# Layer one's last tile of every second chunk selected by TensorE, coefficients kept for eight chunks, degrees summed on VectorE

## The chip, the cores and the metric

One NeuronCore of a Trainium2 chip runs the kernel; nothing is shared with other cores. The metric is the device time of one execution in microseconds, lower is better. Each quoted median is over several executions of the same program on one chip; the profile is one further execution, with its own time.

## What is computed

A graph network over 3125 nodes with 128 features and 100000 edges, sorted by destination. After a layer norm and a relu, two relational layers run one after the other: an edge gathers the row of its source node, weighs it by eight coefficients (one for each basis, from its type, times the edge's norm), and the rows are summed by destination; a dense product with eight basis matrices and a loop weight follows. Then two plain graph convolutions use the edge counts and the degrees of the nodes.

```python
def _rel_layer(h, src, dst, etype, norm, V, comp, loop_w, bias, activation):
    c = comp[etype]
    for b in range(num_bases):                 # 8 bases
        xb = h @ V[b]
        m = m + c[:, b, None] * xb[src]
    agg = segment_sum(m * norm, dst)
    out = agg + bias + h @ loop_w
...
deg = segment_sum(ones, dst)                   # for the two convolutions
norm = rsqrt(deg)[src] * rsqrt(deg)[dst]
```

## The kernel before, in words

Nodes lie in 25 groups of 128. The edges lie in 784 tiles of 128 (782 real ones), eight tiles to a chunk, 98 chunks, four chunks to a group. `relational_layer` is called twice. In the code the first call has `layer == 0`; the texts here call it layer one, and the second call (`layer == 1`) layer two. Every engine runs its own program over groups and chunks, and semaphores join them. Work on an engine is in the order in which the code issues it.

In layer one, for each chunk c = 4g + j:

- GpSimd (L765) starts an indirect DMA for each tile, which fetches 128 rows of `h` into `ring`, a buffer of eight chunks. Before a chunk it waits until TensorE has used the chunk that lay in that slot (`edges_done`). 32 tiles are fetched ahead of the layer, in `prepare` (L280).
- SyncE loads the edge types for a chunk six ahead (`co.load`, L456), and in chunk j = 1 of each group it stores the finished group's slab of edge counts, 800 KB (`store_slab`, L793).
- VectorE builds, in this order: the one-hots of types for chunk c + 6 (L464), the matches of destinations (L868), the one-hots of the source's place in its block (`build_lo`, L874), the weighted matches `C` (`weigh`, L888), the one-hots of block and destination `M` (`build_keys`, L879), and the coefficients of chunk c + 5 (`co.scale`, L479 and L483). `build_lo` waits for TensorE to have begun chunk c - 1 (`m_free`); TensorE waits for `M` of chunk c (`m_ready`), so VectorE is at most one chunk ahead. `keep_deg` (L935) copies a group's degrees in chunk j = 2.
- TensorE first has two register loads (L1100, L1102), then the slab part `sum_slab` (L1002, L1033, L1038, L1041: edge counts in two halves), the coefficient product (L473), and then the edge part (L1124: 16 recorded passes of the gathered rows against `C`, after a wait for the rows' landing and for `c_ready`) with the hand-over to the next bank (L1002 of `ps_z`, L1129). In chunk j = 1, between the register loads and the slab part, `out_and_deg` multiplies the last group's sums by the eight bases (L552 to L554) and sums its degrees by 25 small matmuls of the fp16 counts with ones (L1068). At the end of chunk j = 3 there is one transposition (L543).
- ScalarE copies both sums out of PSUM (L1174, L1184), and finishes the group (L568, L570).

Layer two has a feature that layer one lacks. Of every chunk up to number 87 only seven tiles are gathered. The eighth is selected: SyncE loads its 128 source numbers to all partitions (`load_sources`), VectorE builds 25 blocks of one-hots in two halves (`make_pick`, L910), TensorE multiplies them with the rows of `H`, split once into three bf16 parts by `split_rows` (L897 to L900) (`pick_rows`, L1083: 25 matmuls of 384 columns into one bank), and VectorE adds the three parts into the ring (`keep_picked`, L916).

All coefficients of both layers are made in layer one and lie in two tables of 784 tiles.

## Time and profile before

| | us |
|---|---|
| median of 3 runs | 2128.14 (2127.25 to 2131.23) |
| the profiled execution | 2125.18 |
| its span in the trace | 2123.6 |

| engine | busy us | share of the span |
|---|---|---|
| TensorE (PE) | 1806.7 | 85% |
| its weight loads (PEld) | 1346.7 | 63% |
| GpSimd (POOL) | 1453.1 | 68% |
| VectorE (DVE) | 1190.5 | 56% |
| ScalarE (ACT) | 360.4 | 17% |

The profiled execution took 1.6 us more than its span, and lies 3 us under the median. Layer one runs from about 90 us to 1068 us, layer two from there to about 2020 us, and a short dense stage ends the kernel.
### The profile page before, as it was taken

To read this page: it belongs to the slowest core of one execution; us is meant where nothing else is said; L and a number is where in the kernel's file an instruction comes from. 1 tells how busy PE (TensorE), PEld (TensorE's weight loads), DVE (VectorE), ACT (ScalarE), POOL (GpSimd) and SP (SyncE) were. 2 spreads that over 40 slices of the span, in tenths; PEclk is the share of its full clock that TensorE was granted. 3 is DMA by queue.
4 is the path that set the end of the run, shared out by engine and by line. 5 is a ranking of instruction groups with operands and counts; after the bars stand their busy time and mean duration, and the time that the engine had idled before them with its cause. 6 is when DMAs were issued, how large, how long until landed. Compare 5 with 4: busy or idle time off the path is not lost. (4 is left out here: it accounts for less than half of the span.)

```text
span 2123.6 us, 38749 instructions
## 1 busy us (share of the span) xinstructions
PE 1806.7 (85%) x11730; PEld 1346.7 (63%) x11731; DVE 1190.5 (56%) x2013; ACT 360.4 (17%) x869; POOL 1453.1 (68%) x1573
## 2 busy tenths in 40 slices
PE   1398998989888888887849989889999899978798
PEld 1277777777666676766637766666666666655455
DVE  7565665656555554654267766666666756612433
ACT  2022222222222221222201101001010101101200
POOL 5777777777777777777567777777777777776000
PEclk8555555555555555555579989999999999979899
DMA  5233333232232223223222222223332232334363
GB/s 144 68 78 96 80 80 93 77 98 76 76 95 77 77 77 93 78 74 88 60 65 63 60 59 60 58 83 83 97 88 83 80 95 75 90 92 128 130 216 124
DMA packets 188885, 186.53 MB, mean 88 GB/s; under 512 B 109132, under 2 KB 161085, under 8 KB 188794
## 3 DMA queue, kind: packets, MB, share of 16 engines
q0 software_dynamic: 47232, 96.83, 17.1%
q1 hardware_dynamic: 133510, 84.47, 14.1%
q10 hardware_dynamic: 8052, 4.04, 0.7%
q8 instruction: 55, 0.90, 0.2%
q14 instruction: 36, 0.29, 0.0%
HBM read 159.75 MB, written 25.47 MB: 87 GB/s over the span
## 5 line engine op out<-in xcount | busy, mean ns | idle before, releaser
L765 POOL DMA_INDIRECT ring<-h_rows,rel_idx x1356 | 1305.5, 963 | 425.6 <-issue 394.8
L1124 PE MATMUL rel_ps_z<-rel_C,ring 128*128 128x56 f32 x3128 | 540.5, 346 | 79.7 <-DMA ring<-h_rows,rel_idx 79.2
L1124 PEld LDWEIGHTS rel_ps_z<-rel_C,ring 128*128 128x128 f32 x3128 | 524.8, 260 | 94.4 <-issue 90.4
L1083 PE MATMUL rel_ps_p<-rel_h_parts,rel_pick 128*128 128x384 bf16 x2200 | 391.8, 337 | 48.4 <-DVE rel_h_parts L900 22.0
L910 DVE TENSOR_TENSOR rel_pick<-rel_src_row,dve_bank 128x1664 bf16<-128x1664 int32 (+1 forms) x176 | 319.5, 1816 | 182.8 <-PE rel_ps_p L1083 180.2
L1083 PEld LDWEIGHTS rel_ps_p<-rel_h_parts,rel_pick 128*128 128x128 bf16 x2200 | 217.3, 101 | 200.6 <-issue 66.5
L1184 ACT ACTIVATE rel_ZT<-rel_ps_z 128x304 f32 x292 | 114.2, 426 | 1071.2 <-PE rel_ps_z L1124 1065.7
L874 DVE TENSOR_TENSOR rel_lo<-dve_bank,src_lo_table 128x1024 bf16<-128x1024 f32 x98 | 120.0, 1225 | 235.2 <-PE rel_ps_a L1033 234.8
L1174 ACT ACTIVATE rel_A<-rel_ps_a 128x500 f32 x292 | 165.6, 603 | 454.4 <-PE rel_ps_a L1041 419.9
L464 DVE TENSOR_SCALAR rel_onehot<-rel_types,type_id 100x1024 bf16<-100x1024 uint8 x196 | 141.6, 764 | 166.1 <-DMA rel_types<-edge_types 163.0
L552 PE MATMUL rel_ps_o<-V,rel_ZT 128*128 128x128 f32 x784 | 142.4, 356 | 65.4 <-issue 62.3
L552 PEld LDWEIGHTS rel_ps_o<-V,rel_ZT 128*128 128x128 f32 x784 | 132.5, 264 | 67.3 <-issue 63.7
L879 DVE TENSOR_TENSOR rel_M<-dve_bank,key_table 128x1400 bf16<-128x1400 f32 x98 | 157.4, 1606 | 0.0
L1041 PE MATMUL rel_ps_a<-rel_M,rel_lo 128*128 128x175 bf16 x784 | 153.2, 353 | 1.8 <-DVE rel_M L879 1.8
L888 DVE TENSOR_TENSOR rel_C<-dve_bank,coef 128x448 f32<-128x448 f32 x196 | 121.5, 620 | 34.1 <-PE rel_ps_z L1129 20.7
L473 PE MATMUL rel_ps<-comp_parts,rel_onehot 100*128 100x48 bf16 x1568 | 78.6, 211 | 56.0 <-DVE rel_onehot L464 47.9
L774 POOL DMA_INDIRECT ring<-h_rows,idx_table x88 | 89.7, 1019 | 52.4 <-issue 28.3
L1002 PE MATMUL rel_ps_a<-zero 1*128 1x500 bf16 x196 | 108.3, 553 | 15.0 <-issue 14.9
L473 PEld LDWEIGHTS rel_ps<-comp_parts,rel_onehot 100*128 100x128 bf16 x1568 | 79.2, 118 | 57.5 <-DVE rel_onehot L464 48.2
L1129 PEld LDWEIGHTS rel_ps_z<-rel_C,ring 128*128 128x128 f32 x388 | 78.4, 252 | 39.7 <-issue 26.9
L1015 PE MATMUL rel_ps_early<-early_slot,hp_parts 128*128 128x512 f16 (+1 forms) x441 | 100.4, 388 | 3.0 <-DVE early_sums L931 2.4
L1129 PE MATMUL rel_ps_z<-rel_C,ring 128*128 x388 | 96.5, 322 | 0.0
(206 smaller groups left out, 1282.9 us busy)
## 6 DMA issues: line engine op xcount, KB each, us to landing
ring<-h_rows,rel_idx POOLq DMA_INDIRECT x1356
A_slabs<-rel_A SPq DMA_DIRECT2D x25, 800.0 KB
A_slot<-A_slabs SPq DMA_DIRECT2D x25, 800.0 KB, 4.4
early_slot<-A_slabs SPq DMA_DIRECT2D x18, 896.0 KB, 6.1
rel_types<-edge_types SPq DMA_DIRECT2D x97, 100.0 KB
rel_src_row<-in_src_dram SPq DMA_DIRECT2D x88, 64.0 KB, 3.1
last_slot<-A_slabs SPq DMA_DIRECT2D x4, 512.0 KB, 6.1
ring<-h_rows,idx_table POOLq DMA_INDIRECT x120
```

Of the source, the lines that this page charges most:

```text
L464: ins = self.nc.vector.tensor_scalar(self.onehot[:, s % 2, h, :], self.etype[:, s % 2, :], self.t.type_id[0:RH, h:h + 1], None, ALU.is_equal)
L473: ins = self.nc.tensor.matmul(self.ps[:, e * 6 * NB:(e + 1) * 6 * NB], self.onehot[:, s, h, e * P:(e + 1) * P], flat(self.t.comp[:, h, :, ...
L552: m.matmul(self.bank(g)[:, 0:P], ZT[:, b, :], t.V[self.layer][:, b, :], start=(b == 0), stop=False)
L765: g_.indirect_dma_start(ring[:, s * CHUNK + i, :], None, rows_in, bass.IndirectOffsetOnAxis(ap=idx[which][:, n:n + 1], axis=0)).then_inc(l ...
L879: v.tensor_tensor(M[s][:, :, :], keys.unsqueeze(1).to_broadcast(shape), t.key[:, bass.ds(c * CHUNK, CHUNK)].unsqueeze(2).to_broadcast(shap ...
L888: v.tensor_tensor(C[s][:, :, :, :], match[s].unsqueeze(2).to_broadcast(shape), t.coef[layer][:, bass.ds(c * CHUNK, CHUNK), :].unsqueeze(3) ...
L910: v.tensor_tensor(pick[:, b0:b0 + n, :], src_row[s][:, :].unsqueeze(1).to_broadcast(shape), node_ids[:, b0:b0 + n].unsqueeze(2).to_broadca ...
L1041: ins = m_.matmul(into[:, :, bass.ds(half_at[h][i], TW)], lo[s][:, h * HALF + i, :], keyed(s, h * HALF + i), start=False, stop=(i == HALF ...
L1083: ins = m_.matmul(ps_p[s][:, 0:3 * P], pick[:, b, :], h_parts[:, b, :, :].rearrange("p c n -> p (c n)"), start=(b == 0), stop=(b == SRC_BL ...
L1124: ins = m_.matmul(bank(ps_z[s], NB)[:, :, bass.ds(at[i], TW)], ring[:, first + i, :], C[s][:, i, :, :], start=False, stop=(i == n - 1))
L1129: m_.matmul(bank(ps_z[1 - s], NB)[:, :, 0:1], ring[:, first + CHUNK - 1, :], C[s][:, CHUNK - 1, :, bass.ds(at[CHUNK], 1)], start=False, st ...
L1174: ins = s_.activation(A[into][:, :, bass.ds(column, HN)], half_bank(ps_a[h]), ACT.Copy)
```

## The change

In layer one the last tile of each odd chunk from 5 to 95 (46 of them) is no longer gathered but selected as in layer two: with two buffers for source numbers in place of four, and one PSUM bank. TensorE does the 25 matmuls for chunk c + 1 in the even chunk c, between the coefficient product and the edge part, and its last edge matmul of chunk c + 1 waits for the selected row (`row_ready`). VectorE splits `H` in group 0 (two pieces of five groups in each of the chunks 0 and 1, one in chunk 2), builds one half of the one-hots in the odd chunk before and the other in the even chunk, and adds the three parts in the odd chunk. SyncE loads the source numbers a group ahead, behind a wait for the one-hots made from that buffer (`pick_ready`) and ahead of the slab's store and the next types.

To make room, layer one's coefficients are kept in a ring of eight chunks, and the bank `ps_o` becomes the last quarter of the bank `ps_h`. The 25 small matmuls for the degrees are replaced: VectorE reduces the group's counts over the 25 blocks (3200 fp16 numbers in each partition) at the end of its chunk j = 1, and TensorE does one fp32 matmul of that sum with ones at the start of chunk j = 2. `keep_deg` moves from j = 2 to j = 3, and the last two groups' degrees come after the loop.

```diff
-    def scale(self, eng, m):
+    def scale(self, eng, m, slot=None):
...
+            into = self.t.coef[l][:, bass.ds(m * ET if l or slot is None else slot * ET, ET), :]
...
-        self.ps_o = ctx.enter_context(nc.psum_tensor(f"{name}_ps_o", [P, 512], F32))
+        self.ps_o = self.ps_h[:, 3 * P:4 * P] if layer == 0 and not whole else ctx.enter_context(nc.psum_tensor(f"{name}_ps_o", [P, 512], F32))
...
+        def first_picks(c):
+
+            return isinstance(c, int) and FIRST_PICK <= c < END_PICK and c % 2 == 1
+
+        def number(g, j):
+
+            return 2 * g - 2 + j // 2
+
+        def gathers(s, late=False):
+
+            return CHUNK if late else CHUNK - (1 if layer == 1 else s % 2)
...
-                for i in range(CHUNK if late else GATHERS):
+                for i in range(gathers(s, late)):
...
+                def load_sources(g, j):
+
+                    k, s = number(g + 1, j), j // 2
+                    after(sp, pick_ready, 2 * k - 2)
...
+                        if j % 2 == 1 and not (isinstance(g, int) and not first_picks((g + 1) * CPG + j)):
+                            load_sources(g, j)
...
+            def sum_degrees(q, parity):
+                dve.wait_ge(a_kept, (q * CPG + (CPG + 1)) * 2 if not is_group(q, GROUPS - 1) else HALVES)
+                after(dve, deg_done, q)
+                v.tensor_reduce(deg_sum[:, :], A[parity][:, :, MARGIN:MARGIN + P].rearrange("p b n -> p n b"), AX.X, ALU.add).then_inc(deg_summed, 1)
...
                     if layer == 0:
                         match_nodes(c, s)
+                        if j % 2 == 0 and not (isinstance(g, int) and not first_picks(c + 1)):
+                            make_pick(number(g, j + 1), j // 2, g - 1, (1,))
                         build_lo(c, s)
-                        weigh(c, s)
+                        weigh(c, s, parity * CPG + j)
                         build_keys(c, s)
+                        if is_first and j < 3:
+                            split_rows(split_chains, ((0, 1), (2, 3), (4,))[j])
+                        if j % 2 == 1:
+                            if not (isinstance(g, int) and not first_picks(c)):
+                                keep_picked(number(g, j), 0, (parity * CPG + j) * CHUNK + CHUNK - 1)
+                            ahead = (g, 3) if j == 1 else (g + 1, 1)
+                            if not (isinstance(g, int) and not first_picks(c + 2)):
+                                make_pick(number(*ahead), ahead[1] // 2, ahead[0] - 1, (0,))
...
+                    if layer == 0 and j == 1 and not is_first and not is_last:
+                        sum_degrees(g - 1, 1 - parity)
+                    if layer == 0 and j == 3 and not is_first:
                         keep_deg(g - 1)
...
             if layer == 0:
-                keep_deg(GROUPS - 2)
-                keep_deg(GROUPS - 1)
+                for q in (GROUPS - 2, GROUPS - 1):
+                    sum_degrees(q, q % 2)
+                    keep_deg(q)
...
+            def degrees(q):
+                pe.wait_ge(deg_summed, q + 1)
+                after(pe, deg_kept, q)
+                pe.wait_ge(fin.h_new, min(q + 2, GROUPS) if isinstance(q, int) and q >= GROUPS - 2 else q + 1)
+                m_.matmul(fin.ps_h[:, 2 * P:2 * P + 1], deg_sum[:, :], t.ones[:, 0:1], start=True, stop=True).then_inc(deg_done, 1)
...
                     if layer == 0 and j == 1 and not is_first and not is_last:
-                        out_and_deg(g - 1, 1 - parity)
+                        out(g - 1, 1 - parity)
+                    if layer == 0 and j == 2 and not is_first:
+                        degrees(g - 1)
...
+                    if layer == 0 and j % 2 == 0 and not (isinstance(g, int) and not first_picks(c + 1)):
+                        if is_group(g, 1) and j == 0:
+                            pe.wait_ge(split_done, GROUPS // SPLIT_GROUPS)
+                        pick_rows(number(g, j + 1), 0)
...
+                        if layer == 0 and i == CHUNK - 1 and j % 2 == 1 and not (isinstance(c, int) and not first_picks(c)):
+                            pe.wait_ge(row_ready, number(g, j) + 1)
...
-                        t.coef[0] = left(first_layer, "coef0", [P, TILES, NB], F32)
+                        t.coef[0] = left(first_layer, "coef0", [P, COEF_RING * CHUNK, NB], F32)
```

## Rows read from the trace of the kernel before

**Rows 1.** The page's 40 slices of the span, tenths busy.

```profile
POOL 5777777777777777777567777777777777776000
PEclk8555555555555555555579989999999999979899
```

**Rows 2.** Windows: length; PE, PEld, DVE, ACT, POOL busy us (count); clock; DMA share, GB/s.

```profile
139.00:515.00 376.00, 343.91 (x2341) 280.46 (x2340) 226.44 (x370) 97.77 (x210) 284.21 (x301) 0.56 0.33 85
559.00:1016.00 457.00, 386.85 (x2556) 312.30 (x2554) 243.91 (x398) 107.52 (x231) 347.62 (x368) 0.54 0.31 81
```

**Rows 3.** TensorE's waits, 139 to 515, then 559 to 1016: total us, times, longest.

```profile
PE rel_ps_o L552 <- issue: 28.1, 10, 2.9
...
PE rel_ps_z L1124 <- DMA ring<-h_rows,rel_idx: 34.4, 17, 6.6
```

**Rows 4.** GpSimd's groups of instructions by line, 559 to 1016.

```profile
L765 POOL DMA_INDIRECT ring<-h_rows,rel_idx x352 | 344.4, 978 | 109.6 <-issue 100.8 <-DMA ring<-h_rows,rel_idx 7.0 <-PE rel_ps_z L1129 1.8
```

**Rows 5.** Timeline, TensorE in chunk 1, chunk 97, and VectorE's last degrees: start, length.

```profile
100.35 0.23 PE L1033 MATMUL rel_ps_a<-rel_M,rel_lo 128*128 x1
...
1057.95 0.22 PE L1033 MATMUL rel_ps_a<-rel_M,rel_lo 128*128 x1
...
1068.16 0.16 DVE L935 TENSOR_SCALAR deg<-rel_ps_h 128x1 f32<-128x1 f32 x1 [14.95 <-PE rel_ps_h L1068]
```

**Rows 6.** Timeline of TensorE, from an edge part j = 0 through chunk j = 2.

```profile
464.63 3.64 PE L1124 MATMUL rel_ps_z<-rel_C,ring 128*128 128x56 f32 x16
...
471.96 3.75 PE L552 MATMUL rel_ps_o<-V,rel_ZT 128*128 128x128 f32 x16 [2.80 <-issue]
...
476.36 0.78 PE L1068 MATMUL rel_ps_h<-ones,rel_A 128*128 128x1 f16 x25
477.07 0.38 PE L1002 MATMUL rel_ps_a<-zero 1*128 1x500 bf16 x1
...
478.98 3.49 PE L1124 MATMUL rel_ps_z<-rel_C,ring 128*128 128x56 f32 x16
...
483.29 0.59 PE L1002 MATMUL rel_ps_a<-zero 1*128 1x500 bf16 x1
...
486.53 3.64 PE L1124 MATMUL rel_ps_z<-rel_C,ring 128*128 128x56 f32 x16
...
491.23 0.59 PE L1002 MATMUL rel_ps_a<-zero 1*128 1x500 bf16 x1 [0.18 <-issue]
```

**Rows 7.** Windows: an unbroken stretch of layer one, then of layer two's first selection.

```profile
484.00:488.00 4.00, 4.00 (x34) 3.22 (x32) 3.74 (x4) 1.21 (x2) 3.08 (x4) 0.50 0.35 91
...
1093.00:1097.00 4.00, 4.00 (x13) 1.87 (x14) 0.62 (x1) 0.00 (x0) 3.09 (x4) 0.50 0.16 45
1097.00:1101.00 4.00, 2.13 (x13) 1.08 (x11) 1.83 (x2) 0.00 (x0) 3.08 (x4) 1.00 0.22 57
```

**Rows 8.** Timeline: the first two selections of layer two on TensorE.

```profile
1092.94 6.19 PE L1083 MATMUL rel_ps_p<-rel_h_parts,rel_pick 128*128 128x384 bf16 x25 [22.01 <-DVE rel_h_parts L900]
...
1101.58 4.24 PE L1083 MATMUL rel_ps_p<-rel_h_parts,rel_pick 128*128 128x384 bf16 x25 [2.45 <-DVE rel_pick L910]
```

**Rows 9.** Timeline: an edge part of layer one at the full clock, next chunk's start.

```profile
684.26 1.97 PE L1124 MATMUL rel_ps_z<-rel_C,ring 128*128 128x56 f32 x16
...
688.01 0.59 PE L1002 MATMUL rel_ps_a<-zero 1*128 1x500 bf16 x1 [1.24 <-issue]
```

**Rows 10.** Timeline of VectorE: one-hots, the three parts' sum; groups: a split.

```profile
1099.17 0.56 DVE L916 TENSOR_REDUCE ring<-rel_ps_p 128x128 f32<-128x384 f32 x1 [5.54 <-PE rel_ps_p L1083]
1099.64 3.54 DVE L910 TENSOR_TENSOR rel_pick<-rel_src_row,dve_bank 128x1664 bf16<-128x1664 int32 x2
...
L898 DVE TENSOR_TENSOR dst_table<-H,rel_h_parts 128x640 f32<-128x640 f32 x5 | 4.1, 824 | 0.2
```

**Rows 11.** A long reduction (in `prepare`), and VectorE's types, 139 to 515, by line.

```profile
44.85 2.69 DVE L425 TENSOR_REDUCE pre_bad<-pre_wrong 1x1 f32<-1x2450 f32 x1
...
L464 DVE TENSOR_SCALAR rel_onehot<-rel_types,type_id 100x1024 bf16<-100x1024 uint8 x80 | 57.9, 765 | 73.3 <-DMA rel_types<-edge_types 72.0 <-issue 1.2
```

More of the change, by code:

```diff
@@ L730, in half_bank, with landings @@
             return b[:, 0:SRC_BLOCKS * HN].rearrange("p (a n) -> p a n", n=HN)
-        GATHERS = CHUNK - layer
-        def landings(half, late):
+        def first_picks(c):
[4 more added lines that the diff above has]
+            return CHUNK if late else CHUNK - (1 if layer == 1 else s % 2)
+        def landings(half, s, late=False):
             if layer == 1 and late:
-                return PICKED // 2 * (GATHERS * 16) + (half - PICKED // 2) * (CHUNK * 16)
-            return half * (GATHERS * 16)
+                return PICKED // 2 * (gathers(s) * 16) + (half - PICKED // 2) * (CHUNK * 16)
+            if layer == 0 and s % 2 == 1:
+                return half * (CHUNK * 16) if isinstance(half, int) and half < 3 else half * (gathers(s) * 16) + 2 * 16
+            return half * (gathers(s) * 16)
         @block.gpsimd
@@ L754, in chunk @@
                 landed = (ring_even, ring_odd)[s % 2]
-                hold(pool, landed, landings(m * (SLOTS_RING // 2) + s // 2, late))
+                hold(pool, landed, landings(m * (SLOTS_RING // 2) + s // 2, s, late))
                 if s in (0, 2, 4):
@@ L769, in _ @@
                 landed = (ring_even, ring_odd)[c % 2]
-                hold(pool, landed, c // 2 * GATHERS * 16)
+                hold(pool, landed, landings(c // 2, c))
                 if c == SLOTS_RING - 2:
                     stage(0, SLOTS_RING)
-                for i in range(c * CHUNK, c * CHUNK + GATHERS):
+                for i in range(c * CHUNK, c * CHUNK + gathers(c)):
                     g_.indirect_dma_start(ring[:, i, :], None, rows_in, bass.IndirectOffsetOnAxis(ap=t.idx[:, i:i + 1], axis=0))\
@@ L940, in _ @@
                 make_pick(0, 0, 0)
-                split_rows()
+                split_rows(split_chains, range(GROUPS // SPLIT_GROUPS))
                 match_nodes(0, 0)
@@ L1145, in _ @@
             groups(pe, group)
-            out_and_deg(GROUPS - 1, (GROUPS - 1) % 2)
+            out(GROUPS - 1, (GROUPS - 1) % 2)
+            if layer == 0:
+                degrees(GROUPS - 2)
+                degrees(GROUPS - 1)
             if layer == 1:
```

60 lines of the change are left out of this document (32 added, 28 removed).

## The prediction, made before the changed kernel ran

> **What bounds the kernel now.** I read the page's slices first. In layer one (the first twenty slices) GpSimd stands at an even 7 tenths and TensorE's granted clock at 5 tenths, in layer two at 8 to 9 [rows 1]. The two windows over layer one then show that it isn't one regime [rows 2]. Between 139 and 515 us TensorE passes ten groups in 376 us, 37.6 us each (the ten waits ahead of L552, one for each group, count them); from 559 to 1016 us it takes 457 us for the 352 gathers of eleven groups, 41.5 us each [rows 3, 4]. TensorE's waits say why. In the first stretch it never waits for gathered rows for long enough to be listed; in the second it does so 17 times, 34.4 us in all, which is most of the 11 x 3.9 = 43 us between the regimes [rows 3]. GpSimd meanwhile starts one gather after another: idle time before them is "issue", and a gather costs 457 / 352 = 1.30 us in all [rows 4]. It had chunks in hand when the layer began, TensorE worked that lead off at 37.6 us a group, and since about 530 us GpSimd sets the pace. So the gathers that the change removes are a bound only while TensorE can do a group in less than GpSimd's new time, 30 x 1.30 = 39.0 us. TensorE has 39.0 - 37.6 = 1.4 us a group to spare for two selections, at its present clock. That is the question of the case.
>
> **TensorE's group, part by part** [rows 6]. At 1.2 GHz a slab part with the coefficient product takes 486.53 - 483.29 = 3.2 us, and the edge part until the next chunk begins 491.23 - 486.53 = 4.7 us. The dense product takes 476.36 - 471.96 = 4.4 us, after which the slab part runs at 2.4 GHz and takes 1.9 us (477.07 to 478.98). From the edge part of j = 0 to the dense product pass 7.3 us, of which 2.8 us are idle, "issue": the two register loads stand there while the slab's store is on the DMA queues.
>
> What the change adds and takes there, for each of the 23 groups with selections:
>
> - Two selections. One took 4.2 us at the full clock, and the very first of layer two, which began after an idle stretch, 6.2 us: 13 of its matmuls began in 4 us at 0.50, then the clock was full [rows 7, 8]. All 25 at 0.50 would be 25 x 4 / 13 = 7.7 us. In layer one the engine comes from an edge part that leaves the clock at 1.2 GHz, but the slab part is dense and stands right ahead of the selection. I take the half of that first cold stretch: 2 us for 6 matmuls and 19 at 4.2 / 25 = 0.17, that is 5.2, and 10.4 for two. Bounds 4.2 and 7.7 each.
> - The 25 degree matmuls go: 477.07 - 476.36 = 0.7 us; one fp32 matmul of one column comes, two passes; sixteen passes of 128 columns took 3.75, so two take 0.47 at most, and I take 0.3. Net -0.4.
> - Behind a selection the clock is high. The edge part until the next chunk was 3.75 us at the full clock, of which 1.2 us was "issue" (the register loads now show) [rows 9]. In j = 2 that saves 0.9 us. In j = 0 the same, and the register loads come some 5 us later, towards the end of the slab's store: I take 4.8 us in place of 7.3, -2.5 (bounds 0 and -3.6).
> - For a clock that holds into the next slab part now and then: -0.7 (bounds 0 and -2.6, both slab parts behind a selection at 1.9).
>
> Sum: 37.6 + 10.4 - 0.4 - 0.9 - 2.5 - 0.7 = 43.5 us a group. This is over GpSimd's 39.0, so GpSimd fills its ring and waits for `edges_done`; its 46 spared gathers, 46 x 1.30 = 60 us, are then worth nothing. TensorE's wait for landed rows disappears too, but the time is spent.
>
> **VectorE** was busy 226.4 us in ten groups, 22.6 each [rows 2]. Per group come two pairs of one-hot halves, 2 x 3.54, two sums of three parts, 2 x 0.56 [rows 10], and the degree reduction. No row shows that one; the nearest reduces 2450 numbers in 2.69 us [rows 11], so 3200 take about 3.5 (2.7 if fp16 were quicker by a quarter, 5 if the strided read cost half as much again). Sum 34.3 us, under 43.5. What could make it late is its waits: 7.2 us a group for the types, which queue behind the slab's store [rows 11]. The reduction, one sum and one one-hot half (5.8 us) stand in just that stretch, after `M` of j = 1 and before the one-hots of types, so most of this wait is filled. `keep_picked` in an odd chunk waits for TensorE's selection, and behind it are queued the next one-hot half, the coefficients and the next `build_lo`; TensorE has an edge part and a slab part to do in that time, some 7 us, against some 7 us of VectorE's work. I cost it at nothing, with a bound of 2 us a group. The wait of TensorE for the summed degrees stands ahead of the slab part of j = 2, which waits for `M` of that chunk, made later on the same engine: nothing. `keep_deg` one chunk later is still a chunk ahead of the transposition that waits for it: nothing. SyncE's loads of source numbers (64 KB) stand ahead of the slab's store; the one-hots they wait for were made half a group earlier, and ScalarE's copies of the slab come later anyway: nothing, bound 1 us. The ring of coefficients changes an address, and the shared bank is guarded by waits on copies done two chunks earlier: nothing. ScalarE's wait for the split in group 0: nothing.
>
> **Once.** In group 0 VectorE does five splits of four instructions, 20 x 0.82 = 16.4 us [rows 10], two of them (6.6 us) in each of chunks 0 and 1. With 5.7 us of its own work a chunk it needs 12.3 us where TensorE needs 8: 4.3 us late twice and 1 to 2 us in chunk 2, about 10 us (bounds 5 and 14). At the end of the layer the last group's reduction runs only after the last dense product, since the one buffer must be free: 3.5 us, a matmul and its copy, less the 25 small matmuls, about +4.5 ahead of what follows VectorE's last degrees [rows 5].
>
> **Sum.** Before, chunk 1 to chunk 97 (24 groups) took 1057.95 - 100.35 = 957.6 us [rows 5]. After: 37.6 + 10 for the first and 23 x 43.5 = 1000.5, together 1048.1; +90.5, and +4.5 at the end: +95.0. Layer two and the dense stage keep their code and their data. The profiled execution took 2125.2 (1.6 over its span, 3 under the median of the runs), so 2125.2 + 95.0 = 2220.2. I forecast 2220.
>
> **Rule against row.** TensorE's matmuls fill 4.00 of 4.00 us in the middle of chunk j = 2, and the clock granted there is 0.50, while a selection lifts it from 0.50 to 1.00 [rows 7]. So being busy isn't what keeps the clock up here; edge parts, which mostly load weights for 56 columns, are busy at 1.2 GHz. The Trainium skill, "TensorE: Matmul & The Clock Gate" (section "Why this matters for your kernels"), advises to keep the engine continuously busy and free of idle gaps, to get and hold the full clock. By that rule TensorE, once it is never idle, would run at 2.4 GHz through the whole group; this is the first rival. The row of chunk j = 2 speaks against it.
>
> **Rivals.**
>
> 1. The clock stays up, and GpSimd remains the bound: not slower. Two dense selections a group would lift TensorE to 2.4 GHz for most of it. A group would then be 4 x 1.9 + 4 x 3.75 + 4.4 + 2 x 4.25 + 0.5 = 36.0 us, under 39.0. GpSimd's 46 gathers come off in full, 60 us, the split's 10 us are hidden in its lead, and the end costs 4.5: 2125.2 - 60 + 4.5 = 2070. For it: layer two, with a selection in each chunk, has 8 to 9 tenths [rows 1]. Against it: there a selection comes every chunk and no slab part is built; here an edge part of the odd chunk, at 1.2 GHz in every group of before, stands between. It decides where TensorE's group falls under (957.6 - 47.6 - 4.5) / 23 = 39.4 us, 4.1 under my sum. Chance 0.10, and 0.02 for a time within 0.2% of no change.
> 2. The clock is up around each selection and into the slab parts, but not throughout: 4.45 in place of 5.2 for each selection (-1.5), and both slab parts behind them at 1.9 in most groups (-2.6 in place of -0.7, of which I count -1.2): 43.5 - 2.7 = 40.8 us a group, -62 from the forecast: 2158. For it: a slab part at 1.9 us behind the dense product [rows 6]. Chance 0.13.
> 3. VectorE is late. If the 7.2 us for types stay, and each of the two `keep_picked` waits 2.5 us with work queued behind it, a group is 34.3 + 7.2 + 5 = 46.5 us: +69, 2289. It decides when its waits pass 43.5 - 34.3 = 9.2 us a group; before, it waited 15 us. Chance 0.07.
> 4. The selections run at 1.2 GHz throughout: 7.7 each, +5.0 a group, and the savings behind them (0.9 + 2.5 + 0.7) gone: 52.6, +209, 2429. Against it is the rise within the first selection of layer two [rows 7]. Chance 0.03.
>
> **How the numbers follow.** The forecast has 0.65, rivals 1 to 4 and no change 0.35. Its own bounds: selections at 6.2 give +2.3 a group, +53; at 4.5, -25; the group-0 and store terms +-30. With rival 2 below and the near half of rival 3 above, the range is 2140 to 2285; it leaves out rival 1, no change, rival 4 and part of rival 3, under 0.2. A measurement of this kernel can tell 0.2% (4 us) from no change. Faster by over that: 0.10; within: 0.02; slower: 0.88.
>
> **What the next profile would show.** Layer one ends at about 1163 us in place of 1068. TensorE's wait for landed rows is gone, and GpSimd waits for TensorE's L1129. The selections in layer one last 4.5 to 6 us, with the clock at 0.5 when they begin; the mean clock of the layer rises from 0.55 to 0.65 or more. VectorE is busy 34 us a group and its wait for types shrinks to 2 or 3 us. I would be wrong if TensorE's group took under 39.4 us, which a granted clock over 0.8 in the layer would show, or if VectorE's waits for the types and the selection added up to over 9 us a group.

## The result and the profile after

The changed kernel took 2316.77 us (median of 4 runs, 2311.72 to 2319.32) against 2128.76 for the kernel before beside it: a ratio of 1.088, 95% interval 1.086 to 1.090. The forecast was 2220 with a range of 2140 to 2285. It had the sign right and missed half of the size: +188 us in place of +92, 32 us beyond its range.

The profiled execution took 2319.32 us, its span is 2317.5. Two rows of its page's 40 slices, for [rows 1]:

```profile
POOL 6776656666566665566502777777777777777000
PEclk7566766666666666666675899988999999978899
```

GpSimd falls from 7 tenths to mostly 6 and 5 in layer one, the clock rises from 5 tenths to mostly 6. So the gathers went and, as the waits below show, no longer pace the layer. The waits of the whole layer (175 to 1190 us: total, times, longest), for [rows 3, 4]: TensorE's first, then VectorE's and GpSimd's.

```profile
PE rel_ps_h L555 <- issue: 59.0, 21, 3.1
PE rel_ps_a L1049 <- issue: 42.9, 21, 2.1
PE rel_ps_h L1116 <- ACT H L571: 1.1, 1, 1.1
PE rel_ps_a L1088 <- DVE rel_M L906: 0.8, 1, 0.8
...
DVE ring L945 <- PE rel_ps_p L1131: 193.0, 43, 5.1
DVE rel_lo L901 <- PE rel_ps_a L1080: 34.5, 41, 3.4
...
POOL ring L782 <- PE rel_ps_z L1185: 47.1, 10, 5.3
```

(The last row is of 559 to 1016 us.) TensorE waits for no gathered row, and for VectorE 0.8 us in a thousand. What is left ahead of it are idle stretches that no semaphore explains ("issue"), now twice a group (L555 and L1049), 102 us in all. In the program's order TensorE's register loads stand there, as they do ahead of every chunk; that they are the cause is a reading, since the trace doesn't list them. VectorE and GpSimd wait for TensorE, so TensorE's own sequence sets the layer.

Where the 193.9 us between the spans stand, by the marks of [rows 5]: chunk 1 begins at 106.21 in place of 100.35 (+5.9); from there to chunk 97, at 1236.76, pass 1130.55 us in place of 957.6 (+172.9); from chunk 97 to VectorE's last degrees 17.9 in place of 10.2 (+7.7); behind them 1062.9 in place of 1055.4 (+7.4). The medians differ by 188.0, 5.9 less than these spans; in which stretch the two profiled executions differ from their medians isn't known. The first group took 45.8 us, so the other 23 took 1084.8 / 23 = 47.2 each, against a forecast of 43.5.

One of them, piece by piece, TensorE's timeline (start, length, idle time ahead of it), for [rows 6]:

```profile
609.51 5.19 PE L1131 MATMUL rel_ps_p<-rel_h_parts,rel_pick 128*128 128x384 bf16 x25
614.54 1.89 PE L1180 MATMUL rel_ps_z<-rel_C,ring 128*128 128x56 f32 x16
...
619.72 3.75 PE L555 MATMUL rel_ps_h<-V,rel_ZT 128*128 128x128 f32 x16 [2.74 <-issue]
...
624.41 0.62 PE L1049 MATMUL rel_ps_a<-zero 1*128 1x500 bf16 x1
...
627.68 3.64 PE L1180 MATMUL rel_ps_z<-rel_C,ring 128*128 128x56 f32 x16
...
632.25 0.56 PE L1116 MATMUL rel_ps_h<-ones,rel_deg_sum 128*128 128x1 f32 x2
632.74 0.59 PE L1049 MATMUL rel_ps_a<-zero 1*128 1x500 bf16 x1
...
635.97 5.61 PE L1131 MATMUL rel_ps_p<-rel_h_parts,rel_pick 128*128 128x384 bf16 x25
641.42 1.89 PE L1180 MATMUL rel_ps_z<-rel_C,ring 128*128 128x56 f32 x16
...
645.93 0.59 PE L1049 MATMUL rel_ps_a<-zero 1*128 1x500 bf16 x1 [2.08 <-issue]
```

| piece, start to start | before [rows 6] | after | difference | forecast |
|---|---|---|---|---|
| two selections | none | 5.03 + 5.45 | +10.5 | +10.4 |
| edges of j = 0, to the dense product | 7.33 | 5.18 | -2.15 | -2.5 |
| dense product | 4.40 | 4.69 | +0.3 | 0 |
| degrees (25 small matmuls, then one) | 0.71 | 0.49 | -0.2 | -0.4 |
| slab part of j = 1 | 1.91 | 3.27 | +1.35 | -0.7 |
| edges of j = 1 | 4.31 | 4.57 | +0.25 | with it |
| edges of j = 2 | 4.70 | 4.51 | -0.2 | -0.9 |
| sum | | | +9.8 | +5.9 |

The slab part of j = 1 had run at 2.4 GHz before [rows 6] and doesn't any more: of the first 22 groups it took 1.9 us in 19 before and in 2 after, 3.2 or 3.3 in the others. The windows show where the clock stands (length; TensorE and weight loads busy; VectorE, ScalarE, GpSimd; granted clock; DMA share, GB/s): first and second half of the selection, the edges behind it, the idle stretch, the dense product, the slab part of j = 1.

```profile
609.60:612.00 2.40, 2.40 (x13) 1.20 (x10) 0.85 (x1) 0.92 (x2) 1.79 (x3) 0.60 0.14 39
612.00:614.40 2.40, 2.40 (x17) 1.43 (x16) 0.00 (x0) 0.00 (x0) 1.79 (x3) 1.00 1.06 248
614.60:616.80 2.20, 2.20 (x20) 2.00 (x18) 2.06 (x2) 0.18 (x1) 1.40 (x2) 1.00 0.98 197
616.90:619.70 2.80, 0.08 (x1) 0.02 (x1) 2.66 (x5) 0.46 (x2) 1.37 (x2) 0.76 0.33 104
619.80:624.30 4.50, 4.50 (x20) 4.28 (x21) 4.50 (x2) 0.00 (x0) 3.28 (x5) 0.50 0.18 48
624.50:627.60 3.10, 3.10 (x28) 1.88 (x27) 3.10 (x5) 0.79 (x2) 2.49 (x3) 0.50 0.16 45
```

The clock is up from the middle of the selection and through the edges, 2.2 us of work. Then TensorE stands idle for 2.74 us, the clock falls within that stretch (0.76 over it), and all that follows until the next selection is at 1.2 GHz. An idle stretch of 2.80 us stands there in the kernel before too, and its dense product still ended with the clock up [rows 6]; why it doesn't after a selection isn't shown. The end of the layer, on VectorE, where the last reduction stands behind the last but one group's degrees:

```profile
1247.74 0.16 DVE L969 TENSOR_SCALAR deg<-rel_ps_h 128x1 f32<-128x1 f32 x1 [18.02 <-PE rel_ps_h L1116]
1247.82 6.13 DVE L965 TENSOR_REDUCE rel_deg_sum<-rel_A 128x128 f32<-128x3200 f16 x1
1254.63 0.16 DVE L969 TENSOR_SCALAR deg<-rel_ps_h 128x1 f32<-128x1 f32 x1 [0.68 <-PE rel_ps_h L1116]
```

### The profile page after: what moved, and what is told of

It reads as the page before. It is cut to its first block and busy times, and to the rows that moved or that the text cites. A ratio compares the mean times of both kernels' runs of the same rounds, so it can differ in the third digit from the quotient of the medians.

```text
span 2317.5 us, 40468 instructions
## 1 busy us (share of the span) xinstructions
PE 1983.8 (86%) x12305; PEld 1410.7 (61%) x12306; DVE 1534.7 (66%) x2196; ACT 360.0 (16%) x869; POOL 1406.5 (61%) x1527
## 5 line engine op out<-in xcount | busy, mean ns | idle before, releaser
L782 POOL DMA_INDIRECT ring<-h_rows,rel_idx x1312 | 1259.3, 960 | 531.4 <-issue 429.3
L1131 PE MATMUL rel_ps_p<-rel_h_parts,rel_pick 128*128 128x384 bf16 x3350 | 649.1, 357 | 48.8 <-DVE rel_h_parts L927 22.0
L939 DVE TENSOR_TENSOR rel_pick<-rel_src_row,dve_bank 128x1664 bf16<-128x1664 int32 (+1 forms) x268 | 486.0, 1814 | 182.3 <-PE rel_ps_p L1131 179.8
L1131 PEld LDWEIGHTS rel_ps_p<-rel_h_parts,rel_pick 128*128 128x128 bf16 x3350 | 348.1, 106 | 311.6 <-issue 134.8
L1180 PE MATMUL rel_ps_z<-rel_C,ring 128*128 128x56 f32 x3128 | 466.3, 314 | 38.4 <-DMA ring<-h_rows,rel_idx 38.4
L1180 PEld LDWEIGHTS rel_ps_z<-rel_C,ring 128*128 128x128 f32 x3128 | 459.9, 231 | 50.2 <-issue 42.8
L945 DVE TENSOR_REDUCE ring<-rel_ps_p 128x128 f32<-128x384 f32 x134 | 74.7, 557 | 218.0 <-PE rel_ps_p L1131 215.3
L1049 PE MATMUL rel_ps_a<-zero 1*128 1x500 bf16 x196 | 114.9, 586 | 51.9 <-issue 51.9
L965 DVE TENSOR_REDUCE rel_deg_sum<-rel_A 128x128 f32<-128x3200 f16 x25 | 153.5, 6140 | 0.0
L555 PE MATMUL rel_ps_h<-V,rel_ZT 128*128 128x128 f32 x400 | 93.0, 427 | 64.2 <-issue 63.4
L555 PEld LDWEIGHTS rel_ps_h<-V,rel_ZT 128*128 128x128 f32 x400 | 86.6, 329 | 65.8 <-issue 64.8
```

The source lines that it names most:

```text
L555: m.matmul(self.bank(g)[:, 0:P], ZT[:, b, :], t.V[self.layer][:, b, :], start=(b == 0), stop=False)
L782: g_.indirect_dma_start(ring[:, s * CHUNK + i, :], None, rows_in, bass.IndirectOffsetOnAxis(ap=idx[which][:, n:n + 1], axis=0)).then_inc(l ...
L939: v.tensor_tensor(pick[:, b0:b0 + n, :], src_row[s][:, :].unsqueeze(1).to_broadcast(shape), node_ids[:, b0:b0 + n].unsqueeze(2).to_broadca ...
L965: v.tensor_reduce(deg_sum[:, :], A[parity][:, :, MARGIN:MARGIN + P].rearrange("p b n -> p n b"), AX.X, ALU.add).then_inc(deg_summed, 1)
L1131: ins = m_.matmul(ps_p[s][:, 0:3 * P], pick[:, b, :], h_parts[:, b, :, :].rearrange("p c n -> p (c n)"), start=(b == 0), stop=(b == SRC_BL ...
L1180: ins = m_.matmul(bank(ps_z[s], NB)[:, :, bass.ds(at[i], TW)], ring[:, first + i, :], C[s][:, i, :, :], start=False, stop=(i == n - 1))
```

## The experiments

The theory after the result: TensorE's selections are nearly the whole loss, the reduction is no part of the pace, and the miss of 3.7 us a group comes from where the selection stands, ahead of an idle stretch that wastes the clock it wins. Its rivals: the reduction or the one-hots delay the group; or a selection costs TensorE its time wherever it stands.

Five runs were made where the kernel before takes 2127 to 2131 us; I tell these first. The first four stood beside the same runs of it (2131.45), u1 was made later beside others (2127.34). Group times are from the start of the dense product of group 0 to that of group 22, both read in the timeline, divided by 22; those of before are from its first profile.

| kernel | us | ratio to before, 95% | starts | group |
|---|---|---|---|---|
| before | 2131.45 | | 133.58, 1010.11 | 39.8 |
| r0, the change | 2320.51 | 1.089 [1.086, 1.092] | 147.34, 1194.49 | 47.6 |
| r1, no selection | 2141.27 | 1.004 [1.002, 1.006] | 133.76, 1012.68 | 40.0 |
| r2, degrees on TensorE | 2301.79 | 1.080 [1.078, 1.082] | 147.56, 1185.71 | 47.2 |
| r4, selections behind the edges | 2440.14 | 1.144 [1.142, 1.147] | 148.04, 1310.39 | 52.8 |
| u1, one late selection | 2119.45 | 0.996 [0.995, 0.998] | 148.87, 1007.56 | 39.0 |

**The change again (r0).**

> The changed kernel itself, unedited, as the measure that the three variants beside it are read against. If the chip behaves as in the first comparison, 2312 to 2320 us, a ratio of 1.086 to 1.090 to the kernel before, and groups of 47 to 48 us in layer one. In the four runs of the first set the kernel before itself took 2777 us instead of 2128, with long waits for signals of other engines in the trace; if that comes back, the ratio here tells whether the change costs the same share there: by the theory that TensorE alone sets the pace, the same 6.9 us a group more; by the rival that signals between engines set the pace on such a chip, much less, and the variants can't be told apart by it.

It came out as in the first comparison, 2320.51.

**No selection (r1).** The diff takes away what belongs to selections in layer one, the split of `H` in group 0 too, and leaves the ring of coefficients and the degree sum on VectorE.

```diff
-                        if j % 2 == 0 and not (isinstance(g, int) and not first_picks(c + 1)):
-                            make_pick(number(g, j + 1), j // 2, g - 1, (1,))
...
-                        pick_rows(number(g, j + 1), 0)
...
-            return CHUNK if late else CHUNK - (1 if layer == 1 else s % 2)
+            return CHUNK if late else CHUNK - layer
```

> The same source as e1_no_selection, run beside the change itself. No selection and no one-hots: GpSimd gathers all eight tiles of every chunk in layer one again; the degree sum stays on VectorE and the coefficients stay kept for eight chunks. Theory (the selections' time on TensorE is the cause of all the loss in layer one): the groups fall back to 40 to 40.6 us and the whole to 2132 to 2142 us, the 4 to 14 us above the kernel before being the two reductions at the end of the layer. Rival (the VectorE reduction, 6.14 us once a group, sits in the chain of every group): groups of 42 us or more, 2170 us or more.

2141.27, at the upper end of the theory's range, and far from the rival's 2170. So 179 of the 189 us are the selections with their split. TensorE's wait for gathered rows is back, as in [rows 3] (139 to 1016 us):

```profile
PE rel_ps_z L1160 <- DMA ring<-h_rows,rel_idx: 44.8, 26, 6.5
```

Of the 10 us above before, the reductions at the end of the layer are 8.2: from the start of the last dense product to the last degrees pass 13.0 us, against 4.8. The groups here also show that the fast slab part of j = 1 isn't lost to selections alone: without any, it took 3.3 us in 7 of the first 22.

**Degrees back on TensorE (r2).**

```diff
-                        sum_degrees(g - 1, 1 - parity)
...
+                for b in range(SRC_BLOCKS):
+                    ins = m_.matmul(fin.ps_h[:, 2 * P:2 * P + 1], A[parity][:, b, MARGIN:MARGIN + P], t.ones16[:, 0:1],
+                                    start=(b == 0), stop=(b == SRC_BLOCKS - 1))
```

> The same source as e2_degrees_on_pe, run beside the change itself. Both selections stay, the degrees of a group are summed on TensorE by its 25 small matmuls as in the kernel before, and VectorE's reduction is gone. Theory (TensorE sets the pace, the reduction is off the path except at the end of the layer): the groups stay at 47 to 48 us or grow by up to 0.9, the end of the layer is 7 us shorter, 2305 to 2330 us. Rival (the reduction delays the one-hots or the edges): groups of 44 us or less, 2230 us or less.

2301.79, 3 under the band I had given, and far from the rival. The reduction takes nothing from a typical group: in both kernels most alternate between 47.5 and 48.1 us. Of the 18.7 us the profiled executions show 5.6 at the end of the layer, 9.0 in the 22 groups and 1.2 behind the layer; the rest is between them and the medians. The middle one is a surprise of its own. Five of r2's groups took 44.4 to 46.4 us and all others 47.0 or more, against one of 44.8 in r0 (and two of 44.9 and 45.2 in the first profile of the change). Two groups of r2 in a row, the first short, the second long (dense product and the edges of j = 1):

```profile
236.77 3.50 PE L555 MATMUL rel_ps_h<-V,rel_ZT 128*128 128x128 f32 x16 [2.15 <-issue]
242.66 1.97 PE L1180 MATMUL rel_ps_z<-rel_C,ring 128*128 128x56 f32 x16
...
281.60 3.75 PE L555 MATMUL rel_ps_h<-V,rel_ZT 128*128 128x128 f32 x16 [2.57 <-issue]
289.56 3.64 PE L1180 MATMUL rel_ps_z<-rel_C,ring 128*128 128x56 f32 x16
```

The same instructions: in the short one the clock rises at the end of the dense product, and the edges take 1.97 us; in the long one it doesn't. From the dense product to these edges pass 5.9 or 8.0 us. The windows behind the two dense products (columns as above) have the clock at 1.00 and 0.50:

```profile
241.00:244.00 3.00, 3.00 (x40) 2.55 (x40) 2.71 (x3) 1.21 (x2) 2.39 (x3) 1.00 0.37 104
286.00:289.00 3.00, 3.00 (x16) 1.62 (x16) 1.78 (x3) 0.60 (x1) 2.39 (x3) 0.50 0.44 111
```

That is the clock at work, in one kernel, with nothing else changed; what tips it isn't shown. So one short group says little, and a kernel has to be judged by many.

**Both selections behind the edges (r4).** `pick_rows` moves from ahead of the edge part of an even chunk to behind it. In j = 0 the selection is then followed by the dense product, which the program issues at the start of j = 1 (the expectation puts it ahead of the selection, which is wrong).

```diff
-                    if layer == 0 and j % 2 == 0 and not (isinstance(g, int) and not first_picks(c + 1)):
-                        pick_rows(number(g, j + 1), 0)
                     s, n = sum_edges(g, c, j, at)
...
+                    if layer == 0 and j % 2 == 0 and not (isinstance(g, int) and not first_picks(c + 1)):
+                        pick_rows(number(g, j + 1), 0)
```

> The same source as e4_selection_after_edges, run beside the change itself. The same two selections, each at the end of the even chunk, behind its edge matmuls and dense product, not before them. Theory (of the 47.2 us of a group, about 3.7 come from the place of the selection: the clock that it wins is lost before the dense product and the next slab, and the register load behind it is waited for): groups of 43 to 45 us, 2215 to 2265 us. Rival (the 3.7 us come with a selection wherever it stands, since the sum of TensorE's work is longer and its clock lower): 46.5 us or more, 2300 us or more.

2440.14, 5 us a group slower than the change. By the number this is in the rival's range, but not by its cause, a selection's own time on TensorE. TensorE's waits (175 to 1190 us) show why, and VectorE's timeline where they come from.

```profile
PE rel_ps_a L1088 <- DVE rel_M L906: 126.7, 38, 5.6
PE rel_ps_h L1116 <- DVE rel_deg_sum L965: 43.7, 19, 2.8
PE rel_ps L475 <- DVE coef L486: 28.1, 20, 2.2
PE rel_ps_a L1049 <- issue: 10.1, 12, 1.1
PE rel_ps_h L555 <- issue: 6.6, 9, 0.9
...
615.45 1.60 DVE L906 TENSOR_TENSOR rel_M<-dve_bank,key_table 128x1400 bf16<-128x1400 f32 x1
624.60 0.56 DVE L945 TENSOR_REDUCE ring<-rel_ps_p 128x128 f32<-128x384 f32 x1 [7.55 <-PE rel_ps_p L1131]
...
627.90 6.16 DVE L965 TENSOR_REDUCE rel_deg_sum<-rel_A 128x128 f32<-128x3200 f16 x1
...
638.75 1.60 DVE L906 TENSOR_TENSOR rel_M<-dve_bank,key_table 128x1400 bf16<-128x1400 f32 x1
```

VectorE stands 7.6 us for the selected rows. Behind that wait it has queued the copy, the one-hots, the coefficients, the reduction and then the next masks `M`, which are ready 15.8 us after the selection ended; TensorE waits for them. A wait moved on one engine was moved on the other too, and there the reduction does count. The three waits are 198.5 us in 19.2 groups, 10.3 a group: without them 42.5, which is what the theory wanted, but that is a subtraction and no run. What the trace does show of the theory: the idle stretches ahead of L555 and L1049 are 16.7 us in place of the change's 102, each of the first 22 dense products took 2.4 or 2.5 us (4.7 in the change), and each slab part behind them 1.9 us.

**One late selection, degrees on TensorE (u1).** To take VectorE's queue out, one selection a group instead of two (chunk j = 1's, at the end of j = 0), and no reduction. GpSimd gathers 31 tiles of 32. Three things differ from the change at once, the number of selections, their place and the degrees; r2 prices the degrees, and the timeline has to tell the other two apart.

```diff
-            return isinstance(c, int) and FIRST_PICK <= c < END_PICK and c % 2 == 1
+            return isinstance(c, int) and FIRST_PICK <= c < END_PICK and c % CPG == 1
...
+                    if layer == 0 and j == 0 and not (isinstance(g, int) and not first_picks(c + 1)):
+                        pick_rows(number(g, j + 1), 0)
```

> The kernel of t2_one_late_pe_degrees again, alone, on the chance of a chip on which the kernel before takes 2131 us: theory, groups of about 38 us while TensorE sets the pace and 40.3 us once GpSimd does, 2100 to 2110 us in all; rival, 42.5 us a group or more, 2190 us or more. Where the kernel before takes 2700 us or more, again within 1% of it.

2119.45: faster than the kernel before by 0.4%, interval 0.2 to 0.5, and than the change by about 200 us. The rival (2190 or more) is out; the theory's 2100 to 2110 is missed by 9 us. TensorE's group is 39.0 us, 1.4 over the 37.6 of [rows 3], not 5 over it, where I had 38. GpSimd goes on without a pause and is only a little slower (355 gathers in the 457 us from 559 to 1016, 1.29 each, 39.9 for 31), so that TensorE never worked off its lead and waited for no gathered row. TensorE's timeline:

```profile
606.83 3.64 PE L1176 MATMUL rel_ps_z<-rel_C,ring 128*128 128x56 f32 x16
...
611.21 7.02 PE L1131 MATMUL rel_ps_p<-rel_h_parts,rel_pick 128*128 128x384 bf16 x25
618.06 1.95 PE L555 MATMUL rel_ps_h<-V,rel_ZT 128*128 128x128 f32 x16
...
620.49 0.37 PE L1046 MATMUL rel_ps_a<-zero 1*128 1x500 bf16 x1
...
622.41 1.97 PE L1176 MATMUL rel_ps_z<-rel_C,ring 128*128 128x56 f32 x16
...
626.29 0.76 PE L1114 MATMUL rel_ps_h<-ones,rel_A 128*128 128x1 f16 x25 [1.36 <-issue]
```

and its windows: most of the selection, then the dense product with the slab part.

```profile
613.50:617.50 4.00, 4.00 (x16) 1.95 (x15) 0.00 (x0) 0.00 (x0) 3.06 (x5) 0.57 0.45 116
618.00:622.00 4.00, 4.00 (x35) 3.17 (x34) 3.59 (x8) 0.45 (x1) 3.08 (x4) 1.00 0.21 50
```

This selection is itself slower than the change's, 6.85 us against 5.03, and gets the clock only near its end; in the change a slab part, here an edge part stands ahead of it. Yet from the edges of j = 0 to the dense product pass 11.2 us against 7.3 [rows 6], 3.9 more and not 6.85: the register loads now stand behind the selection in the program, and the idle time of 2.8 us is gone. The dense product takes 2.4 in place of 4.4, and the edges of j = 1 and the slab part of j = 2 0.6 less together. 3.9 - 2.0 - 0.6 = 1.3 us a selection. In the change the selection for the same chunk cost 5.03 - 2.15 + 0.3 + 1.35 + 0.25 = 4.8 by the table. So the pieces next to the selection account for the difference, and they are alike in all of the first 22 groups: the dense product takes 2.4 or 2.5 us, the slab part behind it 1.9. That is the theory of the place, shown for one selection a group; the control, one selection a group at the change's place, wasn't run.

**Runs that told little.** The other runs fell where the kernel before itself takes 2726 to 2781 us. There the waits are of another kind, as in these rows of s2, the same kernel as u1 (139 to 1016 us): ScalarE's waits of up to 18 us, and TensorE's ahead of the edges, neither of which the trace puts down to an engine of the program. u1 has no such row, and its TensorE is busy for 834 of the 877 us, s2's for 656:

```profile
ACT rel_A L1233 <- remote: 222.3, 24, 18.3
PE rel_ps_z L1176 <- issue: 96.4, 90, 2.6
```

| kernel | us | ratio to before beside it, 95% |
|---|---|---|
| e1, as r1 | 2729.86 | 0.983 [0.980, 0.987] |
| e2, as r2 | 2768.02 | 0.997 [0.994, 1.000] |
| e3, selections of 13 matmuls (leaves 12 of 25 blocks out) | 2695.15 | 0.972 [0.968, 0.975] |
| e4, as r4 | 2782.92 | 1.002 [1.000, 1.004] |
| r3, as e3 | 2668.22 | 0.976 [0.970, 0.982] |
| r5, r4 with degrees on TensorE | 2734.71 | 1.001 [0.998, 1.004] |
| r6, s1, t1, v1, r5 with one-hots behind the masks | 2719.98, 2759.11, 2751.17, 2717.60 | 0.996, 0.992, 0.990, 0.994 |
| r7, s2, t2, as u1 | 2717.33, 2760.27, 2714.41 | 0.995, 0.992, 0.996 |

There r2's kernel is level with before, where it is 8% slower elsewhere, so these ratios say nothing of TensorE's pace. The first four, for which I expected times as in the first comparison, and which all missed them:

> The changed kernel without its 46 selections in layer one: all eight tiles of a chunk are gathered, no source numbers are loaded, H is not split there. The ring of coefficients, the shared PSUM bank and the reduction of the degrees on VectorE stay. Theory A (the selections on TensorE cost it all; TensorE paces layer one): the pattern of before comes back, 37.6 us a group and then GpSimd's 41.5, and only the end of the layer is some 8 us later: 2132 to 2142 us. Theory B (the reduction of 6.1 us on VectorE, or the shared bank, slows each group): 2200 us or more stays.

> The changed kernel, with the degrees summed as before by 25 small matmuls on TensorE, now at the start of chunk j = 2, and no reduction on VectorE. VectorE has 6.1 us a group less to do, TensorE about 0.3 us more. Theory A (TensorE paces): 23 x 0.3 = 7 us more in the loop, some 7 us less at the end: 2310 to 2322 us. Theory B (VectorE paces, its wait for the selection being work queued late): at least 3 us a group less, 2250 us or less.

> The changed kernel with 13 of the 25 matmuls of each selection in layer one; the rows of the other twelve blocks are left out of the selected tile. VectorE builds all one-hots as before. Theory A: 46 x 12 matmuls of 0.17 (full clock) to 0.31 us (half) go from the path, 94 to 171 us: 2146 to 2223 us; nearer to the upper end if the clock no longer rises within the shorter selection. Theory B (VectorE paces): 2290 us or more.

> The changed kernel with each selection moved from between the coefficient product and the edge part to the end of the even chunk, behind the edge part and ahead of the next chunk's register loads. Theory A (part of the 47.2 us a group is register loads that show behind a selection, 2.8 and 2.1 us, and a dense product and slab part at half the clock): both go, and each selection starts from a colder clock, 6 us in place of 5.2: 43 to 45 us a group, 2215 to 2265 us. If those idle times are only moved: 2300 us or more.

Three runs of u1's kernel, all within 1% of before and a little under it (0.4% to 0.8%); the groups that theory and rival speak of can't be told apart there:

> One selection a group (for the second chunk), issued behind the edges of the first chunk, so that the dense product, the next slab and the next edges follow it; GpSimd gathers 31 tiles of a group's 32; degrees on TensorE. Theory (the late selection's 5.6 us come back as clock in what follows it, 1.8 in the dense product, 1.8 in the slab, 1.9 in the edges, so TensorE stays at about 38 us and GpSimd at 31 x 1.30 = 40.3 sets the end): 24 x 1.3 = 31 us less than the kernel before and up to 6 more for the split of the rows in group 0, 2100 to 2110 us. Rival (a selection costs TensorE its 5 us wherever it stands, so a group is 42.5 us or more): 2190 us or more.

> The kernel of r7_one_late_pe_degrees again: one selection a group, behind the edges of the group's first chunk; 31 of 32 tiles gathered; degrees on TensorE. Where the kernel before takes 2131 us: theory: TensorE at about 38 us, GpSimd at 31 x 1.30 = 40.3 us sets the end, 2100 to 2110 us. Rival (a selection costs TensorE 5 us wherever it stands): 42.5 us a group or more, 2190 us or more.

> The kernel of s2_one_late_pe_degrees again, alone. Where the kernel before takes 2131 us: theory, groups of about 38 us while TensorE sets the pace and 40.3 us once GpSimd does, 2100 to 2110 us in all; rival, 42.5 us a group or more, 2190 us or more. Where the kernel before takes 2700 us or more: within 1% of it, as in s2, and nothing is told apart.

The kernel with the halved selections and the two late pairs (r5, and r6 with its repeats) ran nowhere else, so their questions stay open. Halved selections:

```diff
-                    for b in range(b0, b0 + n):
+                    for b in range(b0, b0 + (n if layer == 1 else n - 6)):
```

> The change with each selection cut to 13 of its 25 matmuls (7 of 13 in the first half, 6 of 12 in the second); tiles whose sources lie in the other blocks get wrong rows, everything else is as in the change. Same source as e3_half_selection, on a chip where the kernel before takes 2131 us. Theory (TensorE's own work sets the group, so that a group follows the length of the selections): 2 x 2.4 us less a group than 47.2, so 42 to 43 us, 2190 to 2215 us in all; if the shorter selection also leaves the clock low, less is saved and it lands at 44 us, 2235 us. Rival (what costs is that a selection is there at all, with its waits for the one-hots and the register load behind it): 46 us or more, 2290 us or more.

And the pair of late selections without the reduction, then also with the one-hots behind the masks, which would say whether the 42.5 us of r4's subtraction are real:

```diff
                         build_keys(c, s)
+                        if j % 2 == 0 and not (isinstance(g, int) and not first_picks(c + 1)):
+                            make_pick(number(g, j + 1), j // 2, g - 1, (0, 1))
```

> r4_selection_after_edges, which took 2440 us and 52.9 us a group, with its degrees on TensorE as in the kernel before. In the trace of r4 TensorE waits 5.5 us for the masks rel_M, which VectorE builds only behind the selected rows' copy, the next one-hots, the coefficients and the 6.16 us reduction: VectorE's queue is the cause there. Theory: without the reduction the long of the two waits goes (5.5 us) and the short one stays, groups of 46 to 48 us, 2270 to 2310 us. Rival (the late selection itself is slower on TensorE, whatever VectorE does): 52 us, 2420 us or more.

> r5_late_pe_degrees with both halves of a selection's one-hots built behind the masks of the even chunk, not ahead of them; nothing of VectorE's stands then between the selected rows' copy and the next masks but the coefficients and one type one-hot. Theory (a selection placed so that the dense product and the next slab follow it gets back in clock most of what it costs): TensorE's group is 39.5 to 42 us, 2120 to 2180 us. Rival (the clock falls behind a late selection as it did behind an early one, or VectorE stays late): 46 us or more, 2270 us or more.

> The kernel of r6_late_builds_first again: both selections behind the edges of the even chunk, one-hots built behind the masks, degrees on TensorE. Where the kernel before takes 2131 us: theory (the clock that rises in a selection serves the dense product, the next slab and the next edges, so that a selection costs 1 to 3 us net): TensorE's group is 39.5 to 42 us, 2120 to 2180 us in all. Rival (a selection costs its full 5 us and the clock behind it falls as in the change): 46 us or more, 2270 us or more.

> The kernel of s1_late_builds_first again, alone. Where the kernel before takes 2131 us: theory, 39.5 to 42 us a group and 2120 to 2180 us in all; rival, 46 us or more a group and 2270 us or more. Where the kernel before takes 2700 us or more: within 1% of it, as in s1, and nothing is told apart.

> The kernel of t1_late_builds_first again, alone. Where the kernel before takes 2131 us: theory, 39.5 to 42 us a group and 2120 to 2180 us in all; rival (two selections cost TensorE their 10.5 us wherever they stand), 46 us or more a group and 2270 us or more. Where the kernel before takes 2700 us or more: within 1% of it, as in t1, and nothing is told apart.

Of these expectations only the clause for a kernel before of 2700 us or more applies where they ran; it held (0.990 in t1, 0.996 in t2, 0.994 in v1). What made these runs slow was not found. It isn't tied to the chip's number in the record: s1 and s2 (kernel before 2781) and u1 (2127) all bear number 13; whether that was the same chip isn't on record.

## Why the prediction was wrong

- **What bounds the layer: right.** It is TensorE, with GpSimd's spared gathers worth nothing. GpSimd waits for L1185, TensorE for no row, and r1 puts the loss on the selections.
- **The selections: right.** 5.03 and 5.45 us for 5.2 each. Rival 4 (7.7 each, the clock down throughout) is out, and so is rival 2 (4.45 each, and both slab parts at 1.9: they took 3.3 and 3.2).
- **The savings behind them: wrong, and this is the step that failed.** I took -0.9, -2.5 and -0.7, -4.1 in all. They were -0.2, -2.15 and, for the last, +1.35 on the slab part with +0.55 around it. Two things were left out. First, I let the clock "hold into the next slab part now and then" and bounded that by zero loss. But the slab part of j = 1 was at 1.9 us in the 37.6 already [rows 6], so the bound of -2.6 for two slab parts counted one that had nothing left to give, and what that row already had could be lost, and was, in 20 of 22 groups. The bounds of such a term have to include a loss wherever a row of before is at the full clock. A group at either clock stands in r2: 2.1 us from the dense product to the edges of j = 1. Second, behind the edges of j = 2 stood 2.08 us of idle time, not the 1.24 of [rows 9], so that the edges' faster run saved 0.2 us and not 0.9. Of the 3.9 us between +5.9 and the +9.8 of the group shown, 2.6 are the first with the dense product and the edges of j = 1, 1.1 the second with j = 0, and 0.2 the degrees.
- **The place of the selection.** I priced it only where the change puts it, though the question why 2.8 us of "issue" stood ahead of the dense product lay in the same rows. u1 shows what it is worth: 1.4 us net for one behind the edges, in place of some 4.8 for each of the change's two.
- **The sum of the miss.** 193.9 us measured between the spans, 95.0 forecast. Of the 98.9: 23 x 3.7 = 84 in the groups, 4 in group 0 and ahead of it (45.8 + 5.9 for 47.6), 3.2 at the end of the layer, 7.4 behind it.
- **Degrees: the size was off, the place right.** The reduction took 6.14 us, over my bound of 5. In a typical group it costs nothing (r2), as said; at the end of the layer it makes 7.7 for 4.5.
- **VectorE (rival 3): not the bound here.** It waited 193.0 / 43 = 4.5 us for each selection and TensorE 0.8 us for it in all. The sign that the prediction names, VectorE's waits for types and selection over 9 us a group, was just reached (193.0 + 3.7 in 21.5 groups, 9.1) without VectorE being late: waits of an engine that itself waits for the slower one don't show that it is the bound, the slower one's waits for it do. But r4 shows how near it was: with the selection one edge part later it became the bound at once, by the queue behind `keep_picked` that the prediction names, with the reduction in it.
- **The rule on the clock (rival 1): no.** TensorE was busy for 0.90 of the layer, and its clock rose only from 0.55 [rows 2] to 0.65, in this window of the changed kernel:

```profile
175.00:1190.00 1015.00, 910.05 (x5557) 665.67 (x5556) 772.18 (x934) 209.99 (x452) 616.79 (x659) 0.65 0.28 71
```

The stretch from the dense product to the next selection, busy for 16.1 of 16.2 us (619.72 to 635.90), ran at 0.50, and u1, busy for 0.95 of 139 to 1016 us, had 0.64. The Trainium skill, "TensorE: Matmul & The Clock Gate" (section "Why this matters for your kernels"), asks for an engine without idle gaps; u1, which closes the gap behind the selection, agrees with it there (1.00 in the dense product). The stretches just named show that it isn't enough.
- **Layer two** was set at nothing. It is 2 to 9 us longer than in the profile of before in all five runs of the first table, r1 with no selection in layer one among them (1064.0 for 1055.4). Its cause is open.

## What to carry to other kernels

Where TensorE runs at either of its two clocks, price a piece of work with its neighbours: write down for each piece behind it which clock it had, whether an idle stretch lies between, and bound what it can lose as well as gain. In this kernel a dense piece was cheapest directly ahead of work that could use the clock, with no idle stretch between. When such a piece moves, follow the engine that waits for its result: what is queued behind that wait moves as well.

## What the runs showed of the hardware

- A run of 25 matmuls of 384 columns took 4.9 to 6.0 us behind a slab part (the change, r2), and 6.4 to 7.1 behind an edge part (u1, r4), both of which had run at 1.2 GHz; in the one shown of the first kind the granted clock was 1.00 over its second half, in that of the second kind it was 0.57 from 2.3 to 6.3 us after its start.
- A stretch of fp32 products, slab and edge parts in which TensorE was busy for 16.1 of 16.2 us ran at a granted clock of 0.50 throughout.
- A VectorE reduction of 3200 fp16 numbers in each partition, in the order of a strided view, takes 6.14 us (25 times, 153.5 us), 1.9 ns a number; the 2450 numbers of [rows 11] took 1.1 each.
- Groups of one kernel, with the same instructions, took 44.4 to 46.4 us or 47.0 to 48.3 (r2): three short ones in a row at the start and two later, all others long. The 2.1 us between two of them from the dense product to the edges are the clock's.
- The same kernels took 2.1 ms in some runs and 2.7 in others, and the change with its degrees on TensorE, which costs 8% in the first, was level in the second. A ratio from one can't be carried to the other.
